# Causal mask of two small attentions: added by VectorE in PSUM instead of by mask products on TensorE

## The reference

```python
# layer 2 attention: 32 heads of 8 columns, 8 key heads, two score maps
causal = jnp.where(jnp.tril(jnp.ones((S, S), dtype=bool)), 0.0, -1e+30).astype(jnp.float32)
s1 = jnp.einsum('bhqd,bhkd->bhqk', q1, k1) * scale + causal
s2 = jnp.einsum('bhqd,bhkd->bhqk', q2, k2) * scale + causal
a1 = jax.nn.softmax(s1.astype(jnp.float32), axis=-1).astype(q1.dtype)
a2 = jax.nn.softmax(s2.astype(jnp.float32), axis=-1).astype(q1.dtype)
aw = a1 - lam_full * a2
attn = jnp.einsum('bhqk,bhkd->bhqd', aw, v) * (1.0 - LAMBDA_INIT)
...
# attention inside the feed-forward block of layer 2: 16 heads of 16 columns
scores = jnp.einsum('bqhd,bkhd->bhqk', q, k) * scale
scores = jnp.where(causal[None, None], scores, jnp.finfo(scores.dtype).min)
probs = jax.nn.softmax(scores, axis=-1)
out = jnp.einsum('bhqk,bkhd->bhqd', probs, v).reshape(b, s, H)
```

## Time and profile before

| what | value |
|---|---|
| median of 3 runs | 2548.9 us (2547.44 to 2551.47) |
| the profiled execution's own time | 2549.37 us |
| its span in the trace | 2548.1 us |
| TensorE's mean granted clock over the span | 0.873 of full |
| units of `l2a_a_` (first to last largest of a batch) | from 1399.0 to 1659.0 us of the span |
| units of `l2f_a_` | from 2125.2 to 2192.3 us |
| busy share of the span: PE, PEld, DVE, ACT, POOL | 81%, 56%, 61%, 43%, 42% |

### The profile page before, as it was taken

One profiled execution on the slowest core, in us unless ns is written; L12 is line 12 of the kernel. 1 busy time (PEld: TensorE's weight loads), 2 busy tenths in 40 slices (PEclk: granted clock), 3 DMA queues, 4 the chain that ended last, 5 costly groups with the idle time before them and its releaser, 6 DMA issues. The chain is left out here.

```text
span 2548.1 us, 35316 instructions
## 1 busy us (share of the span) xinstructions
PE 2059.2 (81%) x12705; PEld 1435.2 (56%) x12752; DVE 1544.0 (61%) x2880; ACT 1086.2 (43%) x2193; POOL 1074.3 (42%) x1101
## 2 busy tenths in 40 slices
PE   5666759999984999967546888878999988798777
PEld 2333346666763999943414454545777765555445
DVE  6877755554445777756785555544556555456546
ACT  3245626455432445535171354442444434432433
POOL 2766717556546767746543233321233222231000
PEclk8766679999986999978768888889999989989788
DMA  4222210000004565521001000020000000012000
GB/s 145 68 60 60 59 42 20 12 24 12 9 1 157 181 188 184 177 79 56 31 19 39 3 3 3 3 83 26 1 1 1 1 1 2 29 48 106 2 1 17
DMA packets 49868, 124.52 MB, mean 49 GB/s; under 512 B 5632, under 2 KB 18432, under 8 KB 47520
## 3 DMA queue, kind: packets, MB, share of 16 engines
q1 hardware_dynamic: 48160, 118.07, 14.5%
q0 software_dynamic: 1536, 4.20, 0.5%
HBM read 105.07 MB, written 16.12 MB: 48 GB/s over the span
## 5 line engine op out<-in xcount | busy, mean ns | idle before, releaser
L1837 POOL TENSOR_SCALAR l0f_probs<-l0f_probs,l0f_tot 128x128 f32<-128x128 f32 (+1 forms) x256 | 201.8, 807 | 141.7 <-DVE l0f_tot L1784 141.1
L3191 POOL TENSOR_TENSOR l2x_probs<-l2x_probs,l2x_rc 128x512 f32<-128x512 f32 x64 | 66.5, 1040 | 254.9 <-DVE l2x_rc L3092 254.9
L1306 DVE TENSOR_REDUCE l2a_a_max<-ps 128x6 f32<-128x768 f32 x128 | 119.5, 954 | 88.0 <-PE ps L1158 87.4
L1362 POOL TENSOR_SCALAR_AFFINE_SELECT l2a_a_probs<-l2a_a_probs 128x256 f32<-128x256 f32 (+1 forms) x192 | 88.3, 484 | 172.5 <-ACT l2a_a_probs L1268 148.7
L2054 PE MATMUL ps<-l0f_xh,l0f_wh 128*128 128x256 f32 x480 | 146.3, 305 | 0.1
L2171 POOL TENSOR_TENSOR l0f_wl<-l0f_raw,l0f_wh 128x1024 fp32r<-128x1024 f32 x60 | 142.0, 2386 | 0.0
L1708 ACT ACTIVATE l0f_probs<-ps,l0f_neg 128x128 f32<-128x128 f32 (+1 forms) x256 | 104.3, 424 | 87.1 <-DVE l0f_neg L1774 87.1
L2056 PE MATMUL ps<-l0f_xh,l0f_wl 128*128 128x256 f32 x480 | 136.5, 284 | 0.0
L2055 PE MATMUL ps<-l0f_xl,l0f_wh 128*128 128x256 f32 x480 | 136.5, 284 | 0.0
L3032 ACT ACTIVATE l2x_probs<-ps,l2x_neg,l2x_rs 128x256 f32<-128x256 f32 x128 | 71.0, 559 | 145.5 <-DVE l2x_neg L3082 145.4
L700 DVE TENSOR_TENSOR_SCAN l1x_h<-l1x_dA,l1x_dBu 128x512 f32<-128x512 f32 x64 | 116.6, 1860 | 8.6 <-issue 8.6
(11 more groups left out here) (722 smaller groups left out, 5828.0 us busy)
## 6 DMA issues: line engine op xcount, KB each, us to landing
l0f_raw<-in_e_l0f SPq DMA_DIRECT2D x60, 512.0 KB, 4.1
l0x_bc<-scratch_bc SPq DMA_DIRECT2D x32, 512.0 KB, 4.8
l0f_raw_d<-in_e_l0f SPq DMA_DIRECT2D x60, 256.0 KB, 3.0
scratch_rows<-zero SPq DMA_DIRECT2D x1, 3840.0 KB, 18.9
l0f_xb<-scratch_rows SPq DMA_DIRECT2D x15, 256.0 KB, 3.1
scratch_results<-l0f_yb SPq DMA_DIRECT2D x15, 256.0 KB, 2.3
l0f_slab<-in_g_l0f SPq DMA_DIRECT2D x8, 448.0 KB, 3.5
l2f_ew<-in_e_l2f SPq DMA_DIRECT2D x8, 384.0 KB, 3.0
```

Source lines behind the costliest of these rows:

```text
L1306: dve.tensor_reduce(M[:, 2 * half:2 * half + 2, j, :], src.rearrange("p a (c n) -> p a c n", c=NB_), AX.X, ALU.max).then_inc(*unit_max.tick())
L1362: last = pool.affine_select(part, part, [[0, m], [1, P]], ALU.is_ge, 0.0, base=0, channel_multiplier=-1)
L1837: last = pool.tensor_scalar(pr[:, u % 3, a, r], pr[:, u % 3, a, r], tot[:, u % 3, qt, a:a + 1], None, ALU.mult)
```

## The change

The two mask products of each unit (L1158) are removed, and the last score product closes the sum in PSUM. In `largest`, for the causal attentions, VectorE first adds the float32 mask table to the two diagonal blocks of both banks in one instruction (4 x 128 = 512 columns, read from PSUM and written back to PSUM in place), waits for its own result, and then does the same reduction as before. The table is already in SBUF as `k.kf[:, 368:496]`. Nothing else is changed; the steps, the ring and the waits of the other engines stay.

```diff
@@ Kern.__init__
         self.mask_qk = self.kb[:, 128:256]
+        self.mask = self.kf[:, 368:496]
         self.mask_kq = self.kb[:, 256:384]
@@ small_attention, at_pe, unit
                         last = pe.matmul(banks[:, a, at:at + w], QT[z][r, j, qt * P:(qt + 1) * P], KT[z][r, hs.kj(j), 0:w],
-                                         start=qt == 0, stop=not causal and qt == 1)
-                if causal:
-                    for a in range(2):
-                        diagonal = banks[:, a, :].rearrange("p (q n) -> p q n", n=S)[:, :, 0:P]
-                        last = pe.matmul(diagonal, k.identb, k.mask_qk.unsqueeze(1).to_broadcast([P, 2, P]), start=False, stop=True)
+                                         start=qt == 0, stop=qt == 1)
                 last.then_inc(*unit_ps.tick())
@@ small_attention, at_dve, largest
                 src = ring("unit", b, u)[:, :, 0:384] if causal else ring("unit", b, u)
+                if causal:
+                    diagonal = ring("unit", b, u).rearrange("p a (q n) -> p a q n", n=S)[:, :, :, 0:P]
+                    dve.tensor_tensor(diagonal, diagonal, k.mask.unsqueeze(1).unsqueeze(1).to_broadcast([P, 2, 2, P]), ALU.add).then_inc(*vc.tick())
+                    dve.wait_ge(*vc.now())
                 dve.tensor_reduce(M[:, 2 * half:2 * half + 2, j, :], src.rearrange("p a (c n) -> p a c n", c=NB_), AX.X, ALU.max).then_inc(*unit_max.tick())
```

## The result

The changed kernel takes 2658.89 us (median of 4 runs, 2656.41 to 2662.92); the kernel before took 2550.18 us on the same chip (2547.44 to 2555.29). The ratio is 1.0425, with a 95% interval from 1.0404 to 1.0447: 4.2% slower. The forecast was 2632 us with a range of 2600 to 2665; the time lies inside it, near its upper end, and 27 us of the loss have to be explained as well.

A forecast was written before the change was run, and what follows sets the result against it. No engine bounds the whole span; TensorE paces `l2a_a_`'s middle batches. Added times of 51 (middle batches), 7.5 (first), 8 (last) and 16 us (`l2f_a_`), together 82.5 on 2549.4, gave 2632 us, range 2600 to 2665.

The forecast's parts named there:

- The mechanism: Both causal attentions: VectorE, at 1.68 us a unit through the two-slot ring, paces the units; chance 0.84.
- One sign of being right: Profile after: the wait ahead of VectorE's units mostly gone, TensorE's units, weighs and backs waiting for the reduction instead.
- The walk: Step by step timing of a middle `l2a_a_` batch at full clock: 32.7 us with mask products, 39.0 changed.
- the clock: Middle `l2a_a_` batches: granted TensorE clock falls from 0.86 to 0.75, giving 43.75 us a batch.
- its own formula: Middle `l2a_a_` batch: 39.0 us plus 9.5 times the share at half clock, the share being 2 x (1 - clock).
- The terms of the sum: Added time: six middle `l2a_a_` batches 51 us, first batch 7.5, last batch 8, `l2f_a_` 16; together 82.5 us.
- the end for the lowest clock: Both attentions at the half-clock share of `l0a_` (clock 0.63): 46.0 us a middle batch, 2650 us in all.
- a dearer addition: VectorE's addition at 0.98 us instead of 0.69: up to 46 us more, 2678 us.
- all other stretches keep their length to a microsecond or two: Outside the two causal attentions nothing changes, since they stand between barriers; lengths within a microsecond or two.
- TensorE's freed time: Both attentions: the 0.32 us a unit freed on TensorE buys nothing on VectorE's chain.
- the addition hides in VectorE's idle time: Rival for the attentions: TensorE stays the bound and keeps its 51 us saving, 2498 us; chance 0.04.
- the addition is dear: Rival: with GpSimd working beside it the addition takes 0.98 us, 2665 to 2690 us; chance 0.09.

The follow-up runs named there:

- Experiment 4: The changed kernel with the addition covering only 32 of 128 columns of each diagonal block; 2615.25 us, ratio 1.0215 to the kernel before.
- experiment 3: The kernel before with the change made in `l2f_a_` alone, `l2a_a_` left as it was; 2576.50 us, ratio 1.0069 to the kernel before.
- experiment 10: The changed kernel with 53 filling products a batch of `l2a_a_` where its trace shows TensorE waiting for a reduction; 2620.28 us, ratio 1.0269 to the kernel before.
- experiment 7: The kernel before with 16 filling products a batch, only at the turn from one batch to the next; 2547.59 us, ratio 0.9972 to the kernel before.
- experiment 6: The changed kernel with three filling products ahead of each unit and back and the rows, 63 a batch; 2648.45 us, ratio 1.0365 to the kernel before.
- experiment 2: The changed kernel without its addition, so no mask in the search for the largest; 2574.72 us, ratio 1.0058 to the kernel before.
- experiment 1: The changed kernel with the two mask products of each unit put back on TensorE, addition kept; 2692.21 us, ratio 1.0519 to the kernel before.

## Why the prediction came out as it did

**The mechanism.** VectorE's chain through a ring of two slots sets the pace, as forecast: the additions stand in the trace with 0.69 us and a gap of 0.03, VectorE works 29.9 us a batch (30.8 forecast), and TensorE's units, backs and weighs wait for reductions. Experiment 4 shows that the pace follows the addition, experiment 3 that each attention pays for itself. One sign of being right did not come: VectorE's wait for units was to be mostly gone, and it fell only from 87.4 to 78.4 us.

**The walk.** 39.0 us for a batch at full clock; 39.2 measured (experiment 10). For the kernel before 32.7; 33.1 measured (experiment 7). Both measured batches have fillers in them. So at full clock the change costs about 6.1 us a batch (39.2 less 33.1; forecast 6.3).

**The step that was off: the clock.** The prediction took 0.75 for the middle batches and named 0.63 as its worst end; the trace has 0.55 to 0.58 in five of them. With its own formula, 39.0 + 9.5 x 2 x (1 - 0.56) = 47.4 us, against 48.0 us measured (1466.22 to 1706.06 us in five batches). Of the 12.3 us that such a batch lost against 35.7, about 6.1 are the longer chain's and 6.2 the clock's: 48.0 less 39.2 is 8.8, less the 2.6 that the kernel before already paid (35.7 less 33.1). The term was sized from two other attentions, `l0a_` and `l3a_a_`, and the present one fell lower than either (0.63 and 0.66).

**The terms of the sum.** Six batches from the first join to the seventh: 64 us more, 51 forecast. First batch: 9.1, forecast 7.5; it had clock 1.00 before and has 0.72 now. Last: 11.7, forecast 8; at clock 1.00 it took 33.4 us with fillers (experiment 10), so the forecast of 35 us was too long for full clock and too short for the 38.8 us at 0.60. `l2f_a_`: 24.4, forecast 16; its clock went from 1.00 to 0.64 in the last batch, where the term had allowed 1 us for it. Every term is too small. For the middle batches and the last one the runs show the clock as the reason. For `l2f_a_` they don't: with three fillers in experiment 6 its last two batches stood at 0.87 and 1.00 and the four still took 89.1 us, the fillers' own delay among them.

**Where luck helped.** The six batches were summed as if alike, but the second batch of units took only 35.9 us, 3.0 more than before, and not the 43.75 of the sum. This took 8 us off a miss of about 21 in the other five. The stated range held the time only through its margin: the end for the lowest clock was 2650 us, and what lay above it stood for a dearer addition, which did not come; the time is 9 us above that end. And "all other stretches keep their length to a microsecond or two" is right as a sum only: unchanged code behind `l2f_a_` lost 6 us and `l3a_a_` gained 5, each with its clock.

**TensorE's freed time.** "Buys nothing" was not right. Without the addition the freed time is a loss of 0.58% (experiment 2); with it, the freed time gains 0.9% (experiment 1 against the change), 3.3 us in a middle batch at clock 0.56 to 0.60. What it buys in a middle batch at full clock no run shows. The sum did not hang on this, since the walk was made without the mask products.

The Trainium skill ("TensorE: Matmul & The Clock Gate", section "A second HAM failure mode: psum-queue depth-cycling") tells of a kernel whose matmul groups cycle through PSUM with small idle times between them, and whose clock swings between its two levels for it. The traces agree: with more waits between TensorE's items the clock of a middle batch fell from between 0.86 and 0.90 to between 0.55 and 0.58, and with these waits filled it stood at 0.92 to 1.00 (experiment 10).

**The rivals.** That the addition hides in VectorE's idle time had 88 us of waits against 92 us of work in its favour. It fell with the batches of 48 us, and of 39.2 at full clock. The trace shows why a sum of waits is not a place to work in: after the change VectorE still waited 78.4 us for units, in fewer and longer waits behind weighs and turns, where it has nothing to add the mask to. That the addition is dear fell with its 684 to 700 ns.

## What to carry to other kernels

Moving work from the engine that sets the pace to one with idle time pays only if that idle time lies where the work would come; through the ring of two slots here each added step on the reader's side delayed the writer too. (No run had a ring of another size.) Before taking products away from TensorE, read its granted clock in that stage: where it stands between its levels, the products may be what holds it up, and their removal has to be reckoned at the lower clock. A step by step walk at each clock, and a run with filling products placed in the waits, tell the longer chain from the lower clock, as far as the fillers cost nothing themselves. And where two edits are made at once, each should be tried with and without the other: here one of them changed its sign.

## What the runs showed that was not expected

Taking 320 products away and adding nothing made the kernel 0.58% slower (interval 0.39 to 0.78%), while taking the same products away beside the addition made it 0.9% faster. Filling has to be enough and in the right place: against the change, one product ahead of each wait left the clock at 0.60 and cost 1.0%, three raised it to 0.96 and gained 0.6%, and 53 a batch placed by the trace raised it to 0.92 to 1.00 and gained 1.6% (1.0269 against 1.0425). And the clock is not the same for the same code: in one execution of experiment 7, batches with the same list of instructions took 33.1 us at 1.00 and 40.5 us at 0.75.
